# Local attention: division behind the value sums, and outputs turned for the output projection

## The reference

```python
def attn_layer(x, Wqkv, qs, ksc, Wo):          # x (32, 128, 128), already shifted by shift_tokens
    q, k, v = split(x @ Wqkv, 3)               # 16 heads of 64 channels each
    q = l2norm(q) * qs;  k = l2norm(k) * ksc   # then rotary embedding of q and k
    sim = einsum('bhwie,bhwje->bhwij', bq, bk2) * 8.0      # windows of 32, with one window of look-back
    attn = softmax(where(mask, -big, sim), -1)
    out = einsum('bhwij,bhwje->bhwie', attn, bv2)
    return out.reshape(b, n, 16 * 64) @ Wo     # 1024 -> 128
for i in range(6):
    x = attn_layer(shift_tokens(x), ...) + x
    x = ffn_layer(shift_tokens(x), ...) + x    # layer norm, 128 -> 2 x 341, gated GELU, 341 -> 128
```

## Time and profile before

| | |
|---|---|
| median of 3 runs | 4446.3 us (4444.8 to 4446.31) |
| the profiled execution | 4449.52 us, span 4447.7 us |
| mean granted TensorE clock | 0.967 |
| PE busy | 3986.8 us (90%) |
| PEld busy | 3146.8 us (71%) |
| DVE busy | 3672.2 us (83%) |
| ACT busy | 3560.3 us (80%) |
| POOL busy | 3379.8 us (76%) |

### The profile page before, as it was taken

How to read it: one execution, slowest core, us unless ns; L and a number is a source line. 1 busy time by engine, 2 the same in 40 slices (tenths; PEclk the granted TensorE clock), 3 DMA queues, 4 the chain that set the end, 5 groups by cost and what they waited for, 6 DMA issues and landing times.

```text
span 4447.7 us, 138701 instructions
## 1 busy us (share of the span) xinstructions
PE 3986.8 (90%) x49504; PEld 3146.8 (71%) x49504; DVE 3672.2 (83%) x8896; ACT 3560.3 (80%) x11591; POOL 3379.8 (76%) x2461
## 2 busy tenths in 40 slices
PE   7998885999979999889999889999899998899997
PEld 5666664777767777667777667777677776677776
DVE  7998887888868888778888778888688887788886
ACT  6888984888948888748888568888388887588884
POOL 4544447999939999759999579998499996699993
PEclk9999997999999999989999989999899999899999
DMA  3000000000010000010000000000100000000001
GB/s 80 0 0 1 0 0 15 5 0 0 1 39 4 2 0 0 7 33 3 2 0 0 20 21 5 0 0 2 37 4 2 0 0 12 14 6 0 0 0 34
DMA packets 81158, 39.29 MB, mean 9 GB/s; under 512 B 60085, under 2 KB 73267, under 8 KB 80947
## 3 DMA queue, kind: packets, MB, share of 16 engines
q1 hardware_dynamic: 80946, 36.56, 3.2%
HBM read 21.92 MB, written 2.10 MB: 5 GB/s over the span
## 4 chain that ended last, share of the span: by engine, by line
DVE 34%; PE 28%; ACT 22%; issue 12%; POOL 2%; DVEq 1%; DMA 0%; SPq 0%; ACTq 0%; POOLq 0%
ACT pair L966 13%; PE bank L749 6%; PE bank L679 6%; DVE top L1360 5%; DVE prob L1378 5%; PE bank L672 5%; DVE by_cos L1328 5%; ACT prob_t L983 4%; DVE norm L1343 4%; PE pair L823 4%; PE bank L771 4%; DVE by_sin L1336 3%; DVE top L1286 3%; DVE qk_parts L1261 2%; DVE ctx_all L1427 2%
## 5 line engine op out<-in xcount | busy, mean ns | idle before, releaser
L1081 POOL TENSOR_TENSOR rnorm<-norm2g,neg_half 128x16 f32<-128x16 f32 x384 | 1115.5, 2905 | 237.0 <-DVE norm2g L1353 236.5
L1073 POOL TENSOR_TENSOR rotated<-by_cos,by_sin 128x512 f32<-128x512 f32 x768 | 980.8, 1277 | 178.7 <-DVE by_sin L1336 175.1
L966 ACT ACTIVATE pair<-pair,top 128x128 f32<-128x128 f32 x3072 | 1044.0, 340 | 84.7 <-DVE top L1360 51.1
L1093 POOL TENSOR_TENSOR rotated<-rotated,rnorm 128x512 f32<-128x512 f32 x768 | 784.9, 1043 | 0.5
L1328 DVE TENSOR_TENSOR by_cos<-bank,rot_cos 128x512 f32<-128x512 f32 x768 | 531.2, 692 | 276.1 <-PE bank L679 274.1
L679 PE MATMUL bank<-wqkv_high,xt_high 128*128 128x512 f32 (+1 forms) x1536 | 663.1, 432 | 34.1 <-ACT squares L957 34.1
L749 PE MATMUL bank<-prob_t,vout 128*32 128x128 f32 x12288 | 499.2, 280 | 201.8 <-ACT prob_t L983 181.7
L977 ACT ACTIVATE vout<-bank 128x512 f32<-128x512 f32 (+1 forms) x810 | 465.5, 575 | 238.6 <-PE bank L749 230.6
L966 ACT ACTIVATION_READ_ACCUMULATOR pair<-pair,top 128x1 f32 x3072 | 628.6, 205 | 0.0
L1378 DVE TENSOR_TENSOR prob<-pair,rsum 128x512 f32<-128x512 f32 x768 | 531.1, 692 | 41.1
L957 ACT ACTIVATE squares<-bank 128x512 f32<-128x512 f32 x768 | 466.1, 607 | 107.9 <-DVE by_sin L1336 96.0
(11 more groups left out here) (144 smaller groups left out, 8637.8 us busy)
## 6 DMA issues: line engine op xcount, KB each, us to landing
wqkv_sb<-in_L_ffn_Wqkv_dram SPq DMA_DIRECT2D x36, 256.0 KB, 4.1
ctx_all<-y SPq DMA_DIRECT2D x48, 128.0 KB
ctx_all<-y SPq DMA_DIRECT2D x48, 127.0 KB
wo_sb<-in_L_ffn_Wo_dram SPq DMA_DIRECT2D x48, 64.0 KB, 2.1
out_dram<-y SPq DMA_DIRECT2D x8, 256.0 KB, 3.5
w_sb<-in_L_ffn_W_dram SPq DMA_DIRECT2D x6, 341.0 KB, 3.1
w_sb<-in_L_ffn_W_dram SPq DMA_DIRECT2D x12, 64.0 KB
cst<-in_constants_dram SPq DMA_DIRECT2D x1, 582.0 KB, 3.5
```

The costliest lines, as they stand in the source:

```text
L966: last = nc.scalar.activation(at, at, ACT.Exp, bias=top[jl % 2][:, h:h + 1], accum_out=psum_raw[jl % 2][:, h:h + 1])
L1073: nc.gpsimd.tensor_tensor(rotated[j % 4][:, :, :, :], by_cos[j % 2][:, :, :, :], by_sin[j % 2][:, :, :, :], ALU.add).then_inc(c_rot, 1)
L1081: nc.gpsimd.tensor_tensor(rnorm[slot][:, :, :].rearrange("t g n -> t (g n)"), norm2g[slot][:, :, :].rearrange("t g n -> t (g n)"), neg_hal ...
L1093: nc.gpsimd.tensor_tensor(at, at, rnorm[slot][:, i, :].unsqueeze(2).to_broadcast([P, 2 * HG, DH]), ALU.mult).then_inc(c_unit, 1)
```

## The change

The probabilities are no longer divided. The exponentials go straight from PSUM to `prob` in SBUF without an accumulated sum. V is stored with 65 columns per head (`in_rows`, strides of 65 in the buffers `vout`), the 65th of them ones, set once. The value sums have the transposed probabilities as stationary operand and the 65 columns moving, so their result has the queries on the partitions and the row sum in its 65th column; it lies in `sum_ps`, free columns behind `win_ps` in the PSUM pair of the other parity. VectorE takes the reciprocal of those sums and multiplies 4 x 64 columns into `merged` (128x256). Two new transposes turn `merged` (group s−8) into the left half of bank 7, a second ScalarE copy brings it to `out_rows`, and the output projection reads that. Wo stands in its natural order and is loaded by one DMA. Orders change: VectorE does the maxima and the norms ahead of reciprocal and product, ScalarE copies V and outputs ahead of the squares, and the third early MLP step comes after drain step 6 in place of 5.

```diff
-MLP_EARLY = (1, 3, 5, 7)
+MLP_EARLY = (1, 3, 6, 7)
-VOUTS = GROUPS + WIN.value
+SUMMED = DH + 1
...
+        in_rows = [b[:, 0:HG * SUMMED].rearrange("k (n d) -> k n d", d=SUMMED) for b in vout]
+        out_rows = ring("out_rows", 2, [P, 2 * P])
+        merged = ring("merged", 2, [P, 2 * P])
-        psum_raw = ring("psum_raw", 2, [P, HG])
...
-        win_ps = [t[:, :].rearrange("q (e n) -> q e n", e=2)[:, :, 0:2 * P] for t in (pair45, pair12)]
+        win_ps, sum_ps = ([t[:, :].rearrange("q (e n) -> q e n", e=2)[:, :, cols] for t in (pair45, pair12)]
+                          for cols in (slice(0, 2 * P), slice(2 * P, 2 * P + 2 * SUMMED)))
...
-                for h in range(HG):
-                    for half in range(2):
-                        sp.dma_start(wo_sb[PAD * h:PAD * (h + 1), :].rearrange("r (g s c) -> r g s c", g=NG, s=2)[:, :, half, :],
-                                     wo[l].rearrange("(g h s r) c -> h s r g c", g=NG, h=HG, r=PAD)[h, half]).then_inc(s_wo_in, 16)
+                sp.dma_start(wo_sb[:, :].rearrange("r (k c) -> r k c", c=P), wo[l].rearrange("(k r) c -> r k c", r=P)).then_inc(s_wo_in, 16)
...
-                        pe.wait_ge(c_vout, layer * VOUTS + it * STEPS + j)
+                        pe.wait_ge(c_vout, layer * GROUPS + it * STEPS + j)
+                    if has(it * STEPS + j - WIN.out - 1):
+                        pe.wait_ge(c_ot, layer * GROUPS + it * STEPS + j - WIN.out)
...
-                    pe.wait_ge(c_scaled, m + 1)
+                    if has(it * STEPS + j - 1 - WIN.value):
+                        pe.wait_ge(c_merged, m)
+                    pe.wait_ge(c_exp, m + 1)
...
-                    if not here(it, j, 0):
-                        pe.wait_ge(c_vout, layer * VOUTS + it * STEPS + j)
+                    if isinstance(it, int) and m_first(it, j):
+                        pe.wait_ge(c_ones, STEPS)
+                    pe.wait_ge(c_exp, layer * GROUPS + exps_before(it, j))
...
+                    for h in range(HG):
+                        n = h % 2 * 2 + h // 2
+                        last = nc.tensor.matmul(sum_ps[j % 2][:, h // 2, h % 2 * SUMMED:(h % 2 + 1) * SUMMED], prob_t[jl % 2][:, n, :],
+                                                in_rows[jl][:, h, :], start=True, stop=True)
+                    last.then_inc(c_value, 1)
+            def m_first(it, j):
+                return it * STEPS + j == WIN.value
+            def exps_before(it, j):
+                n = it * STEPS + j - WIN.value + 2
+                return min(GROUPS, n) if isinstance(n, int) else n
+            def values_before(it, j):
+                n = it * STEPS + j
+                return min(GROUPS, n) if isinstance(n, int) else n
+            def win_turn_sums(layer, it, j):
+                if here(it, j, WIN.out):
+                    m = layer * GROUPS + it * STEPS + j - WIN.out
+                    pe.wait_ge(c_vout, layer * GROUPS + values_before(it, j))
+                    if has(it * STEPS + j - WIN.out - 1):
+                        pe.wait_ge(c_ot, m)
+                    pe.wait_ge(c_merged, m + 1)
...
-                        for h in range(HG):
-                            at = 2 * P + h * DH + half * PAD
-                            last = nc.tensor.matmul(value_ps[PAD * h:PAD * (h + 1), half * P:(half + 1) * P],
-                                                    vout[jl][:, at:at + PAD], prob_t[jl % 2][:, h % 2 * 2 + h // 2, :],
-                                                    start=True, stop=True, tile_position=(0, PAD * h))
-                    last.then_inc(c_value, 1)
+                        cols = slice(half * P, (half + 1) * P)
+                        last = nc.tensor.transpose(value_ps[:, cols], merged[(j - WIN.out) % 2][:, cols], ident)
+                    last.then_inc(c_oturn, 1)
...
             def win_project_out(layer, it, j):
...
-                    pe.wait_ge(s_wo_in, 16 * 2 * HG * (layer + 1))
+                    pe.wait_ge(s_wo_in, 16 * (layer + 1))
...
-                    if not here(it, j, 0):
-                        pe.wait_ge(c_vout, layer * VOUTS + it * STEPS + j)
+                    pe.wait_ge(c_ot, m + 1)
...
-                        last = nc.tensor.matmul(acc_ps[:, 0:P], vout[(j - 1) % STEPS][:, half * P:(half + 1) * P], wo_sb[:, k * P:(k + 1) * P],
+                        last = nc.tensor.matmul(acc_ps[:, 0:P], out_rows[j % 2][:, half * P:(half + 1) * P], wo_sb[:, k * P:(k + 1) * P],
...
             def win_step(layer, it, j):
...
+                win_turn_sums(layer, it, j)
...
-                        pe.wait_ge(c_scaled, (layer + 1) * GROUPS)
+                        pe.wait_ge(c_merged, (layer + 1) * GROUPS)
...
+                    if has(it * STEPS + j - WIN.exp - 2):
+                        act.wait_ge(c_pturn, m - 1)
...
-                        at = win_ps[jl % 2][:, h // 2, h % 2 * P:(h % 2 + 1) * P]
-                        last = nc.scalar.activation(at, at, ACT.Exp, bias=top[jl % 2][:, h:h + 1], accum_out=psum_raw[jl % 2][:, h:h + 1])
+                        last = nc.scalar.activation(prob[jl % 2][:, h, :], win_ps[jl % 2][:, h // 2, h % 2 * P:(h % 2 + 1) * P], ACT.Exp,
+                                                    bias=top[jl % 2][:, h:h + 1])
...
             def win_copy_values(layer, it, j):
-                fresh, summed = here(it, j, 0), here(it, j, WIN.value)
-                if fresh or summed:
-                    if fresh:
-                        act.wait_ge(c_vproj, layer * GROUPS + it * STEPS + j + 1)
-                    if summed:
-                        act.wait_ge(c_value, layer * GROUPS + it * STEPS + j - WIN.value + 1)
-                    cols = slice(0 if summed else 2 * P, 4 * P if fresh else 2 * P)
-                    nc.scalar.activation(vout[j][:, cols], value_ps[:, cols], ACT.Copy).then_inc(c_vout, 1)
+                if here(it, j, 0):
+                    act.wait_ge(c_vproj, layer * GROUPS + it * STEPS + j + 1)
+                    nc.scalar.activation(in_rows[j][:, :, 0:DH], value_ps[:, 2 * P:4 * P].rearrange("t (n d) -> t n d", d=DH), ACT.Copy).then_inc(c_vout, 1)
+            def win_copy_sums(layer, it, j):
+                if here(it, j, WIN.out):
+                    m = layer * GROUPS + it * STEPS + j - WIN.out
+                    act.wait_ge(c_oturn, m + 1)
+                    nc.scalar.activation(out_rows[j % 2][:, :], value_ps[:, 0:2 * P], ACT.Copy).then_inc(c_ot, 1)
...
             def win_copy_probs(layer, it, j):
...
             def win_step(layer, it, j):
...
+                win_copy_values(layer, it, j)
+                win_copy_sums(layer, it, j)
...
-                win_copy_values(layer, it, j)
...
+            for b in in_rows:
+                pool.memset(b[:, :, DH:SUMMED], 1.0).then_inc(c_ones, 1)
...
             def win_recip(layer, it, j):
-                if here(it, j, WIN.scale):
-                    m = layer * GROUPS + it * STEPS + j - WIN.scale
-                    jl = (j - WIN.scale) % STEPS
-                    dve.wait_ge(c_exp, m + 1)
-                    nc.vector.reciprocal(rsum[jl % 2][:, :], psum_raw[jl % 2][:, :]).then_inc(c_rsum, 1)
-            def win_scale(layer, it, j):
-                if here(it, j, WIN.scale):
-                    m = layer * GROUPS + it * STEPS + j - WIN.scale
-                    jl = (j - WIN.scale) % STEPS
+                if here(it, j, WIN.value):
+                    m = layer * GROUPS + it * STEPS + j - WIN.value
+                    dve.wait_ge(c_value, m + 1)
+                    nc.vector.reciprocal(rsum[j % 2][:, :].rearrange("q (e i) -> q e i", e=2).unsqueeze(3),
+                                         sum_ps[j % 2].rearrange("q e (i d) -> q e i d", d=SUMMED)[:, :, :, DH:SUMMED]).then_inc(c_rsum, 1)
+            def win_merge(layer, it, j):
+                if here(it, j, WIN.value):
+                    m = layer * GROUPS + it * STEPS + j - WIN.value
...
-                    if has(it * STEPS + j - WIN.scale - 2):
-                        dve.wait_ge(c_pturn, m - 1)
-                    nc.vector.tensor_tensor(prob[jl % 2][:, :, :].rearrange("q (e i) k -> q e i k", e=2), win_ps[jl % 2].rearrange("q e (i k) -> q e i k", i=2),
-                                            rsum[jl % 2][:, :].rearrange("q (e i) -> q e i", e=2).unsqueeze(3).to_broadcast([P, 2, 2, P]), ALU.mult).then_inc(c_scaled, 1)
+                    if has(it * STEPS + j - WIN.value - 2):
+                        dve.wait_ge(c_oturn, m - 1)
+                    nc.vector.tensor_tensor(merged[(j - WIN.value) % 2][:, :].rearrange("q (e i d) -> q e i d", e=2, i=2),
+                                            sum_ps[j % 2].rearrange("q e (i d) -> q e i d", d=SUMMED)[:, :, :, 0:DH],
+                                            rsum[j % 2][:, :].rearrange("q (e i) -> q e i", e=2).unsqueeze(3).to_broadcast([P, 2, 2, DH]),
+                                            ALU.mult).then_inc(c_merged, 1)
...
```

(18 more changed lines are left out.)

## The result

| | before | after |
|---|---|---|
| median | 4446.09 us (4 runs, 4444.8 to 4446.31) | 4663.36 us (4 runs, 4662.76 to 4669.18) |
| ratio | | 1.0492 [1.0474, 1.051] |
| profiled execution | 4449.52 us, span 4447.7 | 4663.08 us, span 4661.3 |
| mean granted clock | 0.967 | 0.970 |

A forecast was written before the change was run, and what follows sets the result against it. A round of handoffs was taken to set the 4.08 us step, TensorE alone needing 3.80; 3.80 + 0.32 + 0.22 = 4.34, +0.26 over 726 steps, 189 us, plus 1 once: 4636 us, range 4530 to 4705.

The forecast's parts named there:

- Value sums: TensorE's value-sum stage: eight full-width records at 0.111 us, limited by weight loads, 0.89 against 0.57, +0.32 us per step.
- Rival A: Value sums: the load does not bound, 0.06 us for 128 columns; step 4.00, 4388 us; chance 10%.
- Turning the outputs: Two more FP32 transposes on TensorE in each step, before the V projection, at 0.11 us each: +0.22 us.
- Softmax division: Lighter DVE product, no accumulator reads on ACT: each gains some 0.3 us per step, worth nothing once TensorE is the limit.
- (a): Value sums' wait for ACT's copy `prob_t`: in time by 0.4 us.
- (b): The output projection's (Wo) wait for the copied outputs: in time by 1.0 us.
- (c): The next probability transposes' wait for DVE's merged outputs: in time by 0.2 us at worst.
- Rival D: The merge arrives late, wait (c) fails and TensorE idles 0.2 us more per step: 4.54, 4780 us; chance 7%.
- Drain: Seven groups per layer summed without projections: extra work hides in idle time; 0 taken, between −3 and +4 us per layer.
- Once and free: Eight memsets of ones cost 1 us on POOL; eight Wo loads become one, covered by the MLP, zero.
- B: A tie: pace about 0.08 or one transpose hidden, handoffs still set the step, 4.05 to 4.10, 4446 us; chance 4%.
- C: Part of the price absorbed: shape switches vanish, turns overlap probability transposes; step 4.15 to 4.26, about 4535 us; chance 9%.

The follow-up runs named there:

- e5: The kernel before with only VectorE's order changed, row maxima and norms ahead of reciprocal and product: 4368.36 us, 0.9825 of the kernel before.
- e10: The kernel before with only the row maxima moved up on VectorE, right after the rotary products: 4347.27 us, 0.9782 of the kernel before.
- e2: The changed kernel with 33 moving columns in place of 65 in each value-sum matmul, a probe leaving out channels 0 to 31 of every head: 4675.02 us.
- e6: The changed kernel with the value sums in F32R, 66 columns and one record pair per matmul in place of two: 4414.95 us, 0.9928 of the kernel before.
- e1: The changed kernel with 128 moving columns in place of 65 in each value-sum matmul: 4681.31 us, 1.0532 of the kernel before.
- e3: The changed kernel with each of its two output transposes done twice: 4803.61 us, 1.0811 of the kernel before.
- e8: The changed kernel with VectorE's order put back, reciprocal and merge ahead of clamp, norms and maxima: 4998.67 us, 1.1241 of the kernel before.
- e4: The kernel before with only the third early MLP step moved from after drain step 5 to after drain step 6: 4465.52 us, 1.0049 of the kernel before.

## Why the prediction was right, point by point

*What bounds the kernel.* That no engine was full, that a round of handoffs set 4.08 and that TensorE alone needed 3.80: right. The changed kernel, where TensorE does not wait, bears out the 3.80: 4.347 less the 0.31 and 0.21 below is 3.83. e5 and e10 took the step of the kernel before to 3.98 and 3.96 by order alone. The text did not name the link of the round that was late; it was the maxima.

*Value sums, +0.32.* The stage is 0.94 in place of 0.89: seven distances of 0.112 and a first one of 0.161. The head transposes behind it fell from 0.50 to 0.44. The tile shape no longer changes ahead of them, but that this is the cause is not shown: in e2 they take 0.47 with no change of shape. Together +0.31, and e6 has half as many records take half as long. The size was right; the reason given for it, the load as the limit, is in part argued. e1 and e2 rule out the moving side. The 0.111 itself was worked out from the lengths of loads of two tile shapes, and that it met the pace is partly luck: the transposes' loads last 140 ns, and their records start 0.109 apart all the same, so the recorded length of a load does not give its pace. Rival A's 0.06, taken from those 140 ns, falls with it. What carried the forecast was the 0.11 measured between L771's records.

The Trainium skill ("TensorE: Matmul & The Clock Gate", LDWEIGHTS) ties the time of a load to its stationary columns alone. The traces agree as far as they go: the loads of e1 and e2 start 0.111 us apart with 128 moving columns and with 33, and in the MLP of the kernel after the loads of 85 columns last some 152 ns, those of 128 some 193. By the 81 ns that the same page of the Trainium skill has for a pair (Back-to-back issue gap), the stage would be an estimated 0.65 us. The 0.94 measured is against that figure for FP32.

*Turning the outputs, +0.22.* 0.57 for six transposes against 0.36 for four, +0.21; e3's second pair +0.209.

*Softmax division, nothing.* ACT's first exponential to the next copy is 1.10 us, where it was 1.39 and 1.01 in the first phase; the two 256-wide copies start 0.28 apart:

```profile
904.64 1.14 ACT L998 ACTIVATE prob<-pair,top 128x128 f32<-128x128 f32 x4
905.74 0.60 ACT L1017 ACTIVATE prob_t<-bank 128x512 f32<-128x512 f32 x1
906.32 0.38 ACT L1005 ACTIVATE vout<-bank 128x256 f32<-128x256 f32 x1
906.60 0.38 ACT L1011 ACTIVATE out_rows<-bank 128x256 f32<-128x256 f32 x1
```

The relief is real, and worth nothing here, because TensorE sets the step. By busy time for each step of the 200 us it is 178.33/49 − 155.54/46 = 0.26 us on ACT and 172.95/49 − 154.02/46 = 0.18 on DVE; the text had some 0.3 for each.

*The new waits.* (a) The copy ends at 906.34 and the value sums start at 906.77: 0.43, forecast 0.4. (b) `out_rows` is written at 906.98 and Wo starts at 908.16: 1.2, forecast 1.0. (c) The merge was given 0.2 at worst:

```profile
904.20 0.42 DVE L1414 TENSOR_TENSOR merged<-pair,rsum 128x256 f32<-128x256 f32 x1
```

It ends at 904.62 and the next probability transposes start at 905.11, 0.5 to spare. Rival D did not come in the steady stretch. e8 shows that it was near in another form: with the merge ahead of norms and maxima the same wait of DVE costs 0.44 a step. In the drain the merge does come late, as told below.

*POOL.* I wrote that its wait for `norm2g` would grow. It fell, from 16.4 to 12.0 in 200 us; the growth is in another wait, for `by_sin` (16.5). POOL's idle time went from 18.8 to 28.9 in 200 us as expected, but at another place.

*The step and its sum.* 4.347 against 4.34. 726 × (4.347 − 4.083) = 192 us, forecast 189.

*Drain, nothing, −3 to +4 a layer.* This term was mis-sized and makes nearly all of the miss. From the mask starts of the traces the whole difference of the spans can be laid out, in us over all six layers. With everything counted from 0, mask start n lies in step n + 5; value sums begin with step 7 and projections end with step 127, so the full steps run from mask start 2 to 123:

| | before | after | difference | e4 |
|---|---|---|---|---|
| start of the span to the first scores | 725.4 | 725.1 | −0.3 | 726.5 |
| fill, mask starts 0 to 2 | 39.9 | 38.7 | −1.2 | 40.6 |
| full steps, mask starts 2 to 123 | 2959.4 | 3151.6 | +192.2 | 2958.4 |
| drain steps, mask starts 123 to 127 | 118.5 | 123.2 | +4.7 | 118.5 |
| last scores to the next layer's first, five times | 521.6 | 536.4 | +14.7 | 535.6 |
| last scores of layer six to the end | 82.9 | 86.3 | +3.4 | 85.1 |

The full steps hold 192.2 us, where 189 were forecast. The last three rows, drain and MLP, hold 22.8, 3.8 for each layer, where nothing was forecast and +4 was the bound. e4, which moves the MLP step and nothing else, has 16.2 in the same rows. (The columns are one profiled execution each; by these the spans of e4 and the kernel before are 16.9 apart, by the medians 22.) So the larger part goes with the moved step, "one drain step later", though the reverse, the changed kernel with the MLP step put back, was not run. The other 6.6 are the change's own, 4.7 of them in the drain steps, where e4 has nothing: there the new work is not wholly hidden.

A stall in the drain of layer one shows one place, rows of DVE and PE of the kernel after:

```profile
1270.65 0.42 DVE L1414 TENSOR_TENSOR merged<-pair,rsum 128x256 f32<-128x256 f32 x1
1271.18 1.09 PE L744 MATMUL bank<-cst,prob 128*128 128x128 f32 x4 [3.30 <-issue]
...
1273.62 1.97 PE L757 MATMUL pair<-vout,prob_t 128*128 128x65 f32 x8
```

TensorE stands for 3.30 us. Its transposes start 0.11 us after the merge has ended (1271.07), and it is the last of what they need: this is wait (c), missed in the drain, with 3.55 us of the MLP's norm and the maxima ahead of the merge on DVE. The value sums behind it take 1.97 instead of 1.11: the granted clock is 0.91 from 1267 to 1271 and 0.50 from 1271 to 1280, so they run at 1.2 GHz and not at 2.4. The same place has a gap in the kernel before too, of 2.37 us, for `prob`, with the clock falling behind it (1.00 from 1230 to 1240, 0.66 from 1240 to 1250). Over the span behind the first 735 us the lower level holds 213 us before and 208 after, so the 22.8 are not longer time at 1.2 GHz.

*Once and free.* The single Wo load takes 10.2 us to land (median of six), and no stage waits for it.

*Rivals.* A and B needed a pace below 0.079 and about 0.08; it is 0.11 at every width tried. C needed a part of the price absorbed; the shorter head transposes gave 0.06 back, and the longer distance behind the first record took 0.05. D did not come in the full steps. The range was to leave out no more than 2 in 10; A, B and D make 21 in 100, and the lower part of C (4.15 is 4497) lies outside it too.

## A version that beats both

e10 is the kernel before with the row maxima moved up: 4347.27 us, 0.9782 [0.9765, 0.9798] of the kernel before, and some 7% below the change. One step of it on PE:

```profile
901.52 0.65 PE L749 MATMUL bank<-prob_t,vout 128*32 128x128 f32 x16
...
904.77 0.50 PE L722 MATMUL pair<-qk_t 64*64 64x64 f32 x16
905.33 0.42 PE L749 MATMUL bank<-prob_t,vout 128*32 128x128 f32 x8
```

905.33 − 901.52 = 3.81, where the earlier trace rows has 905.42 − 901.21 = 4.21: 0.40 of the 0.55 us that handoffs took of such a step is back. On the mean it is 4.083 − 3.957 = 0.13 of 0.28, so some waiting is left.

## What to carry to other kernels

Price a full-width FP32 matmul by its two records when the moving side is narrow, 0.11 us each with 128 stationary columns here: swapping operands to save elementwise work is then paid for by TensorE. When every engine is some 90% busy and one waits a little in every step, follow that wait back to the first operation of its chain and look at what stands ahead of *that* in its in-order queue: one line moved gave 2.2%, where relieving two engines of 150 and 206 us gave nothing, as TensorE got the work in return. An operation that waits long for another engine goes last in its queue, and one at the head of a long chain goes first: that is what e8 and e10 show in this kernel.

## What the runs showed that was not expected

- A record of FP32 value sums keeps 0.11 us from 33 to 128 moving columns; only the first one of a stage shows the width (e1, e2).
- Sixteen records in four column tiles (0.57 us) do in less time what eight of full width do (0.94): the records of the four tiles start 7 ns apart, and a load lasts 109 ns against 191.
- DVE's 128x128 product of the MLP's norm lasts up to 1783 ns in the drain, against a median of 336, while POOL is busy (L1143 and L1145, from 1266.31 to 1269.33). Four of them in the kernel after (columns as in the earlier trace rows):

```profile
1266.37 3.55 DVE L1465 TENSOR_SCALAR ctx_all<-ctx_all,mv,rstd 128x128 f32<-128x128 f32 x4 [1.12 <-POOL rstd L1139]
```

They stand on DVE ahead of that late merge, and the kernel before has the same 3.55 us. Whether POOL is the cause was not tried.
